# A routed FFN on one core: each batch's weight matrix fetched by its own DMA, a table's residue moved to VectorE, the first loads cut smaller

## What is computed

```python
W = weights[condition]
h = jnp.einsum('bct,bcd->bdt', x, W)
flat = h.reshape(T, H)
logits = jnp.einsum('th,eh->te', flat, router_weight) + router_bias
scores = jax.nn.softmax(logits, axis=-1)
topk_w, topk_idx = jax.lax.top_k(scores, K_TOP)
w_sum = topk_w.sum(axis=-1, keepdims=True)
w_dense = jnp.zeros((T, E), dtype=scores.dtype).at[jnp.arange(T)[:, None], topk_idx].add(topk_w)
bias_mix = jnp.einsum('te,eh->th', w_dense, expert_bias)
out = flat * w_sum + bias_mix
x = x + out.reshape(B, S, H)
```

## Time and profile before

| quantity | value |
|---|---|
| median of three runs | 578.3 us (577.3 to 578.7) |
| the profiled execution, its own time | 578.7 us |
| its span, first to last instruction | 576.9 us |
| PE busy | 555.4 us, 96% of the span |
| DVE, POOL, ACT busy | 81%, 68%, 63% |
| DMA engines | 265 GB/s over the span, 81.6% of 16 engines' time |
| share of PE in the chain that ended last | 92% |
| `w_all` from issue to landing | 14.8 us, 3% of the chain |

### The profile page before, as it was taken

How to read it: one execution, slowest core, us unless ns; L and a number is a source line. 1 busy time by engine, 2 the same in 40 slices (tenths; PEclk the granted TensorE clock), 3 DMA queues, 4 the chain that set the end, 5 groups by cost and what they waited for, 6 DMA issues and landing times.

```text
span 576.9 us, 12865 instructions
## 1 busy us (share of the span) xinstructions
PE 555.4 (96%) x3360; PEld 477.3 (83%) x3360; DVE 468.6 (81%) x1054; ACT 362.9 (63%) x772; POOL 392.5 (68%) x456
## 2 busy tenths in 40 slices
PE   5859999999999999999999999999999999999997
PEld 5748888888888888888888888888888888888865
DVE  2558888888888888888888888888888888888874
ACT  3457666767656676666676766667666667676552
POOL 0276677676668667667767766866766776776676
PEclk9879999999999999999999999999999999999999
DMA  8964988788988888998888998888899877889235
GB/s 307 312 148 183 285 270 258 282 266 283 313 257 277 269 272 277 297 268 279 260 284 266 279 314 256 277 264 277 281 295 288 263 266 277 271 270 315 121 147 218
DMA packets 61794, 152.81 MB, mean 265 GB/s; under 512 B 5266, under 2 KB 35986, under 8 KB 53650
## 3 DMA queue, kind: packets, MB, share of 16 engines
q1 hardware_dynamic: 61778, 152.62, 81.6%
HBM read 85.49 MB, written 67.11 MB: 265 GB/s over the span
## 4 chain that ended last, share of the span: by engine, by line
PE 92%; DMA 3%; ACT 1%; DVE 1%; issue 1%; SPq 1%; POOL 0%; POOLq 0%; ACTq 0%; DVEq 0%
PE zt_ps L314 20%; PE xt_ps L302 14%; PE p_ps L362 12%; PE p_ps L367 11%; PE p_ps L364 10%; PE p_ps L363 10%; PE p_ps L368 10%; DMA w_all<-L_cond_weights 3%; PE scores_ps L337 2%; PE scores_ps L346 1%; PE scores_ps L328 1%; DVE e_kept L558 1%; SPq L242 0%; ACT expert_hl L487 0%; ACT x_hi L435 0%
## 5 line engine op out<-in xcount | busy, mean ns | idle before, releaser
L658 POOL TENSOR_TENSOR x_lo<-x_sb,x_hi 128x512 fp32r<-128x512 f32 x256 | 325.7, 1297 | 138.6 <-ACT x_hi L435 137.8
L427 ACT CAST xt_hi<-xt_ps 128x512 fp32r<-128x512 f32 x256 | 149.4, 585 | 142.7 <-PE xt_ps L302 140.7
L513 DVE TENSOR_TENSOR xt_lo<-xt_ps,xt_hi 128x512 fp32r<-128x512 f32 x256 | 173.4, 678 | 77.5 <-ACT xt_hi L427 77.4
L579 DVE SCALAR_TENSOR_TENSOR out_sb<-p_ps,w_sum,x_sb 128x512 f32<-128x512 f32 x256 | 188.5, 736 | 11.7 <-PE p_ps L368 9.9
L435 ACT CAST x_hi<-x_sb 128x1024 fp32r<-128x1024 f32 x128 | 134.1, 1048 | 0.2 <-PE p_ps L368 0.2
L314 PE MATMUL zt_ps<-xt_hi,router_hl 128*128 128x256 f32 x512 | 129.7, 285 | 2.6 <-DVE xt_lo L513 2.5
L314 PE MATMUL zt_ps<-xt_lo,router_hl 128*128 128x256 f32 x512 | 129.2, 285 | 0.0
L302 PE MATMUL xt_ps<-ident,x_sb 128*128 128x128 f32 x784 | 118.9, 277 | 4.3 <-DVE xt_lo L513 4.3
L362 PE MATMUL p_ps<-x_hi,w_hl 128*128 128x512 f32 x256 | 119.6, 467 | 1.9 <-issue 0.5
L314 PEld LDWEIGHTS zt_ps<-xt_hi,router_hl 128*128 128x128 f32 x512 | 98.2, 192 | 8.6 <-DVE xt_lo L513 3.0
L302 PEld LDWEIGHTS xt_ps<-ident,x_sb 128*128 128x128 f32 x784 | 94.7, 144 | 12.7 <-DVE xt_lo L513 4.8
(11 more groups left out here) (40 smaller groups left out, 367.0 us busy)
## 6 DMA issues: line engine op xcount, KB each, us to landing
out<-out_sb SPq DMA_DIRECT2D x126, 512.0 KB, 3.9
x_sb<-x SPq DMA_DIRECT2D x62, 1024.0 KB, 6.6
x_turn<-x SPq DMA_DIRECT2D x120, 128.0 KB, 6.1
x_sb<-x SPq DMA_DIRECT2D x4, 512.0 KB, 6.9
out_sb<-L_ffn_expert_bias SPq DMA_DIRECT2D x2, 512.0 KB, 8.1
out<-out_sb SPq DMA_DIRECT2D x4, 256.0 KB, 2.5
x_sb<-L_ffn_router_weight SPq DMA_DIRECT2D x1, 512.0 KB, 5.2
bias_sb<-L_ffn_router_bias SPq DMA_DIRECT2D x1, 32.0 KB, 14.3
```

Source lines behind the costliest of these rows:

```text
L427: act.copy(xt_hi[:, n % 2, :, r, :], xt_ps[v % 4][:, :].rearrange("p (q c) -> p q c", c=P)).then_inc(xt_hi_ready, 1)
L513: dve.tensor_tensor(xt_lo[:, n % 2, :, r, :], xt_ps[v % 4][:, :].rearrange("p (q c) -> p q c", c=P), xt_hi[:, n % 2, :, r, :].bitcast(F32) ...
L579: dve.scalar_tensor_tensor(out_sb[:, r, cols], p_ps[n % 2][:, :], w_sum[:, o % 2, r:r + 1], x_sb[:, (2 * o + r) % XRING, cols], ALU.mult, ...
L658: pool.tensor_tensor(x_lo[:, r, cols], x_sb[:, (2 * o + r) % XRING, cols], x_hi[:, r, cols].bitcast(F32), ALU.subtract).then_inc(x_lo_read ...
```

## The change

SP no longer loads all 16 matrices. For each batch it reads the number into a register and loads the one matrix, 64 KB, straight into a ring `w_sb` of eight places, right behind that batch's `x` (`load_weights`). ACT makes the rounded high part in slot 3 of the step in which the batch is new (`w_high`), and POOL subtracts for the low part (`w_low`); POOL's copies and its reads of the number are gone. The table's low part is made by DVE behind slot 6 of step 1, and ACT rounds the table in slot 4 instead of 5. The router comes in two halves and the first half of each of the first two batches in two pieces, interleaved, and the batch numbers come before the rest of them.

```diff
-            sp.dma_start(router_sb, router_weight).then_inc(router_loaded, 16)
-
-            for h, landed in ((0, first_half_loaded), (1, x_loaded)):
-                for r in range(2):
-                    cols = slice(h * HALF, (h + 1) * HALF)
-                    sp.dma_start(x_sb[:, r, cols], x[r, :, cols]).then_inc(landed[r], 16)
-            load(0, 1, 0)
-            load(0, 1, 1)
+            def load_weights(m, o, r):
+                b = 8 * m + 2 * o + r
+                place = (2 * o + r) % WRING
+                s = sp.value_load(cond_sb[0:1, bass.ds(b, 1)], min_val=0, max_val=S - 1)
+                sp.dma_start(w_sb[:, place, :], weights[bass.ds(s, 1), :, :].rearrange("a c d -> c (a d)")
+                             ).then_inc(w_loaded[place], 16)
+            sp.dma_start(router_sb[:, 0:HALF], router_weight[:, 0:HALF]).then_inc(router_loaded[0], 16)
+            load_first(0, slice(0, PIECE), first_loaded)
+            sp.dma_start(router_sb[:, HALF:T], router_weight[:, HALF:T]).then_inc(router_loaded[1], 16)
+            load_first(1, slice(0, PIECE), first_loaded)
             sp.dma_start(cond_sb[:, :], condition).then_inc(cond_loaded, 16)
-            sp.dma_start(w_all[:, :, :], weights.rearrange("s c d -> c s d")).then_inc(w_loaded, 16)
+            for r in range(2):
+                load_first(r, slice(PIECE, HALF), second_loaded)
+            for r in range(2):
+                load_first(r, slice(HALF, T), x_loaded)
+            sp.wait_ge(cond_loaded, 16)
+            for r in range(2):
+                load_weights(0, 0, r)
+            for r in range(2):
+                load(0, 1, r)
+            for r in range(2):
+                load_weights(0, 1, r)
...
                     for r in range(2):
                         load(m, i, r)
+                        load_weights(m, i, r)
...
-                pe.wait_ge(w_ready, 4 * i + 4)
+                pe.wait_ge(w_hl_ready, 2 * i + 2)
...
+            def w_high(m, o, r):
+                b = 8 * m + 2 * o + r
+                act.wait_ge(w_loaded[(2 * o + r) % WRING], 16 * (m + (2 * o + r) // WRING + 1))
+                wait(act, p_ready, PIECES * (b - 7))
+                act.copy(w_hl[:, (2 * o + r) % 8, 0, :], w_sb[:, (2 * o + r) % WRING, :]).then_inc(w_hi_ready, 1)
...
-                    if i == 1 and v == 5:
+                    if new and v == 3:
+                        for r in range(2):
+                            w_high(m, i, r)
+                    if i == 1 and v == 4:
...
+                    if i == 1 and v == 6:
+                        dve.wait_ge(expert_hi_ready, 1)
+                        dve.tensor_tensor(expert_hl[E:2 * E, :], expert_sb[E:2 * E, :],
+                                          expert_hl[E:2 * E, :].bitcast(F32),
+                                          ALU.subtract).then_inc(expert_ready, 1)
...
-                s = pool.value_load(cond_sb[0:1, bass.ds(b, 1)], min_val=0, max_val=S - 1)
-                for place in (full, w[:, 0, :]):
-                    pool.tensor_copy(place, w_all[:, bass.ds(s, 1), :].rearrange("p a d -> p (a d)")).then_inc(w_ready, 1)
-                pool.wait_ge(w_ready, 2 * b + 2)
-                pool.tensor_tensor(w[:, 1, :], full, w[:, 0, :].bitcast(F32),
+                pool.wait_ge(w_hi_ready, b + 1)
+                pool.tensor_tensor(w[:, 1, :], w_sb[:, (2 * o + r) % WRING, :], w[:, 0, :].bitcast(F32),
                                    ALU.subtract).then_inc(w_hl_ready, 1)
```

More of the change, by code:

```diff
@@ L44 @@
 XRING = 8
+WRING = 8
 UNROLL = 4
@@ L125, in adaln_router @@
         x_loaded = [sem(f"x_loaded{i}") for i in range(XRING)]
-        first_half_loaded = [sem(f"first_half_loaded{i}") for i in range(2)]
+        first_loaded = [sem(f"first_loaded{i}") for i in range(2)]
+        second_loaded = [sem(f"second_loaded{i}") for i in range(2)]
         x_turn_loaded = [sem(f"x_turn_loaded{i}") for i in range(2)]
@@ L129, in adaln_router @@
         last_stored = sem("last_stored")
-        router_loaded = sem("router_loaded")
-        w_loaded = sem("w_loaded")
+        router_loaded = [sem(f"router_loaded{i}") for i in range(2)]
+        w_loaded = [sem(f"w_loaded{i}") for i in range(WRING)]
         expert_loaded = sem("expert_loaded")
@@ L249, in _ @@
                 sp.dma_start(expert_sb[r * E:(r + 1) * E, :], expert_bias).then_inc(expert_loaded, 16)
-            load(0, 2, 0)
-            load(0, 2, 1)
+            for r in range(2):
+                load(0, 2, r)
+            for r in range(2):
+                load_weights(0, 2, r)
             load_turned(0, 2)
@@ L258, in _ @@
                 load(0, 3, r)
+                load_weights(0, 3, r)
                 if r == 0:
@@ L289, in transposes @@
                     return
-                if first(m, o) and n == 0:
-                    pe.wait_ge(first_half_loaded[r], 16)
+                if first(m, o) and n < PH:
+                    pe.wait_ge((first_loaded, second_loaded)[n][r], 16)
                 if n == (PH if first(m, o) else 0):
@@ L333, in score @@
                 i = 4 * m + o
-                pe.wait_ge(w_ready, 4 * i + 4)
+                pe.wait_ge(w_hl_ready, 2 * i + 2)
                 pe.wait_ge(z_ready, i + 1)
                 for r in range(2):
-                    last = pe.matmul(logits_ps[:, r * E:(r + 1) * E], w_sb[:, (2 * o + r) % 4, :],
+                    last = pe.matmul(logits_ps[:, r * E:(r + 1) * E], w_sb[:, (2 * o + r) % WRING, :],
                                      z_sb[:, r, :], start=True, stop=True)
@@ L626, in _, with w_low @@
                                pattern=[[-1, P]], channel_multiplier=1).then_inc(ident_ready, 1)
-            pool.wait_ge(cond_loaded, 16)
-            pool.wait_ge(w_loaded, 16)
-            def pick_weights(m, o, r):
+            def w_low(m, o, r):
                 b = 8 * m + 2 * o + r
                 w = w_hl[:, (2 * o + r) % 8, :, :]
-                full = w_sb[:, (2 * o + r) % 4, :]
-                wait(pool, logits_in_ps, 4 * m + o - 1)
-                wait(pool, p_ready, PIECES * (b - 7))
-                s = pool.value_load(cond_sb[0:1, bass.ds(b, 1)], min_val=0, max_val=S - 1)
-                for place in (full, w[:, 0, :]):
-                    pool.tensor_copy(place, w_all[:, bass.ds(s, 1), :].rearrange("p a d -> p (a d)")).then_inc(w_ready, 1)
-                pool.wait_ge(w_ready, 2 * b + 2)
-                pool.tensor_tensor(w[:, 1, :], full, w[:, 0, :].bitcast(F32),
-                                   ALU.subtract).then_inc(w_hl_ready, 1)
-            def expert_low():
-                pool.wait_ge(expert_hi_ready, 1)
-                pool.wait_ge(w_hl_ready, 4)
-                pool.tensor_tensor(expert_hl[E:2 * E, :], expert_sb[E:2 * E, :],
-                                   expert_hl[E:2 * E, :].bitcast(F32), ALU.subtract).then_inc(expert_ready, 1)
-                pool.wait_ge(expert_ready, 1)
+                pool.wait_ge(w_hi_ready, b + 1)
+                pool.tensor_tensor(w[:, 1, :], w_sb[:, (2 * o + r) % WRING, :], w[:, 0, :].bitcast(F32),
+                                   ALU.subtract).then_inc(w_hl_ready, 1)
             def x_low(m, o, r):
@@ L666, in step @@
                     for r in range(2):
-                        pick_weights(m, i, r)
-                if i == 1:
-                    expert_low()
+                        w_low(m, i, r)
                 if mid:
```

10 lines of the change are left out of this document (6 added, 4 removed).

## The result

The changed kernel takes **575.18 us** (median of 6 runs, 573.34 to 576.62) against 578.46 (577.30 to 579.46, 6 runs): a ratio of **0.9945, 95% interval 0.9923 to 0.9968**. It is faster by 3.3 us where 5.2 were forecast. The profiled execution took 575.43 us, its span 573.6.

A forecast was written before the change was run, and what follows sets the result against it. PE bounds the loop (16.97 of 17.02 us busy), so only its waits before the loop can shrink. The table's earlier landing and chain start its last transposes 5.2 us earlier: 578.7 - 5.2 = 573.5, or 573.1 against the median; range 571.0 to 575.6.

The forecast's parts named there:

- The queue ahead of the table: DMA queue before the loop: the table's second load lands at 23.6 us instead of 26.0.
- the weights': DMA queue: dropping the 1 MB load saves 3.9 us, four 64 KB loads cost 1.0; table 2.9 earlier.
- the front: Router in halves, x in pieces: PE starts 0 to 1 us earlier, ending in the same join; counted as nothing.
- The stop: SP waits for and reads the batch numbers before issuing further loads; queue loss taken as 0.5 us.
- The chain behind the cast: ACT and DVE, from the table's cast at 23.6 to PE's last transposes at 33.2; DVE's low part 2.4.
- The clock: PE's half clock after the old waits (0.50 from 36.5 to 43.3) stays, since PE idles as long.
- Rival 3: PE's clock stays up after the shorter waits: 2.4 us more gained, 570.7; chance 0.08.
- Rival 1: Table lands at 26.0 as before, by SP's stop or dear small loads: gain 2.8, 575.5 us; chance 0.13.
- the row: PE's last transposes ahead of step 2: start at 33.2 instead of 38.45 us, 5.2 earlier.
- Rival 2: DVE's table instruction waits for POOL's four x_lo on the shared port: 3.7 us lost, 576.8; chance 0.08.
- Rival 4: In the loop e_kept loses its 0.20 us lead over POOL's x_lo and waits: up to 609 us; chance 0.05.
- the loop: Added casts, number reads and loads per step cost nothing; a step still takes 17.02 us.

The follow-up runs named there:

- e3: The changed kernel with the table's low part back on POOL, behind step 1's weights, instead of on DVE: 576.78 us, ratio 0.9977.
- e5: The changed kernel with the old front (router whole, first x in halves) and the batch numbers loaded as the very first transfer: 571.11 us, ratio 0.9876.
- e9: The changed kernel, front in pieces kept, with the batch numbers loaded as the very first transfer: 576.75 us, ratio 0.9971.
- e1: The changed kernel with the old front: router loaded whole, first x in halves, then the batch numbers: 573.94 us, ratio 0.9931.
- e6: The kernel before with only the weights' part (a load per batch, casts on ACT, low parts on POOL), old front and table: 576.22 us, ratio 0.9959.
- e11: e5 with the table's cast on POOL instead of ACT: 570.30 us, ratio 0.9865.

## Why the prediction was right in sign and off in size

- **The queue ahead of the table** (landing at 23.6): the step that failed, by 3.9 us (by 3.1 in e3, with the same queue). Of its terms, the weights' held: without stop and with the old front the table lands at 23.1 (e5), 2.9 before its old time, as 3.9 less 1.0 has it. By the rule on small transfers of the Trainium skill, DMA: Bandwidth & Descriptors, Rules for kernel authors, the four loads would have cost 2.0 (the prediction's estimate); e5 speaks for 1.0. The term that was wrong is the front, "in the same join: nothing": it was weighed only for when PE starts (4.97 instead of 6.10), and never as work of the queue. It costs 4.6 us of the landing where the numbers come first (e9 against e5), 0.3 to 1.8 where they stand in the middle (changed and e3 against e1 and e6). The stop was taken as 0.5. It costs 2.6 with the old front, where less is queued behind the numbers (e1 against e5); in the changed kernel the front hides it, and what it would be there alone no run tells.
- **The chain behind the cast**: 9.25 for 9.6, the low part on DVE 2.29 for 2.4, `e_kept` 0.21 for 0.2. Right. The Trainium skill, GPSIMD Engine Reference, 3.1 Elementwise, has 4497 ns on GpSimd and 2293 ns on VectorE for a `tensor_tensor` of 2048 fp32 elements; the rows agree, with 4.54 us and 2.29.
- **The clock**, kept at half as before: wrong in place, and by luck in my favour, by 1.75 us. PE's long idle time now ends at 32.24 (3.93 us), the half clock passes over transposes that wait for DVE anyway, and at the last row PE has idled only 0.32. Rival 3 had the price of this (2.4) and not the cause: the clock fell all the same, after a longer wait, only in another place. It had 0.08 because I asked whether PE idles as long, and not where.
- **Rival 1** (the table as late as before, 575.5) came out in the time, but its cause, SP's stop, did not: e9. That 575.18 lies near it is 3.5 us lost on the row and 1.75 won on the clock. That it lies in the range at all is luck: without the 1.75 it would be 576.9 (estimate).
- **Rival 2**: DVE's low part did start among POOL's `x_lo`, and it was POOL that waited: DVE's instruction began at 33.64, POOL's second `x_lo` at 33.73, and that one took 3.33 us where it takes 1.3 in the loop; six took 9.58 us there and 7.70 in the loop. That the later of the two is blocked for a whole instruction agrees with the Trainium skill, SBUF — State Buffer, SBUF: two separate sides, as cited in the prediction.
- **Rival 4 and the loop**: a step takes 17.04 us (17.02 before, and from step 1's score to the end the kernels agree within 0.7 us), `e_kept` still starts 0.21 ahead of POOL's `x_lo` (288.42 against 288.63), the DMA share is 0.89 where 0.90 was estimated, and `w_high` waits 1.60 us for weights that come at 13.57, not 11.5, and that costs nothing, since the table's join comes later. Right.

## What to carry to other kernels

Price every load of a prologue twice: by whom it lets start earlier, and by how long it holds all that is queued behind it; the second was the larger here. A value that the issuing engine itself must read is safest at the very front of its queue: with the old front the queue ran dry while it was read (2.6 us), with the new one its place made no difference (e9). And when a wait can't be removed, try it where the tensor engine has slack behind it: where the half clock lay on the projections, these runs took 1 to 2 us longer from row to score.

## What the runs showed of the hardware that was not expected

- Loads to 64 partitions moved at about half the rate of loads to 128, with the engines as busy. While the table moves, the kernel before has 231 GB/s at a share of 1.05, and 426 at 1.02 for `x` alone. The Trainium skill, SBUF — State Buffer, Door 1: The DMA port swizzle, says that partitions 0 to 63 reach 8 of 16 ports and so about half the bandwidth; its section on two DMAs to both halves says that two loads, one to either half, go hardly faster. These rows agree. The router is such a load too (64 rows). Whether that is why its halves, set between pieces of `x`, cost so much, no run shows.
- With the small interleaved loads the parts of later loads land further apart. In the records of the changed kernel the sixteen parts of `x`'s second piece land from 8.10 to 10.14, in e1 those of the first half from 8.09 to 8.56; by step 1's `x` the spread is 3.7 us (17.02 to 20.69). A load is there when its last part is. But in e3, with the same queue, that spread is 1.4 us (17.48 to 18.89) and the table still landed at 26.7; that the spread is what makes the table late is not shown.
- SP takes about 1.1 us from one weight load to the next (4.98 and 6.10 in e5), of which the issue is 0.34: reading one number costs it some 0.75.
- A cast on POOL held up a small instruction of DVE: `neg_max` took 1.08 us instead of 0.17 in e11.
